# Residual stored into an accumulator over the gate's row, first registers loaded in batches, and another order between the feed-forward stage and the expert tiles

## What is computed

```python
sa, ca, ga, sb, cb, gb = (mod[:, 0], mod[:, 1], mod[:, 2], mod[:, 3], mod[:, 4], mod[:, 5])
ga = (2 * (ga >= 0) - 1) * jnp.maximum(jnp.abs(ga), 0.25)
gb = (2 * (gb >= 0) - 1) * jnp.maximum(jnp.abs(gb), 0.25)
h = _layernorm(x, axis=-1) * (1 + ca) + sa
x = x + ga * attn_ref(h, ...)
h = _layernorm(x, axis=-1) * (1 + cb) + sb
x = x + gb * ffn_ref(h, ...)
```

```python
scores = jax.nn.softmax(x @ gate_weight.T, axis=-1)
topk_weight, topk_idx = jax.lax.top_k(scores, TOP_K)
y = jnp.zeros_like(x)
for e in range(N_EXPERTS):
    w_e = jnp.sum(jnp.where(topk_idx == e, topk_weight, 0.0), axis=-1)
    y = y + w_e[:, None] * _glu_ffn(x, gate_up_weights[e], down_weights[e])
y = y + _glu_ffn(x, shared_gate_up, shared_down)
```

## Time and profile before

| | us |
|---|---|
| median of 3 runs (lowest, highest) | 366.6 (365.7, 367.72) |
| the profiled execution | 365.12 |
| its span in the profile | 363.3 |
| mean granted clock of TensorE | 0.948 |
| start of the first expert product (L1773) | 223.50 |

### The profile page before, as it was taken

The page is one execution under the profiler, slowest core; times in us unless marked ns, Lnnn a source line. Parts: engine busy times, 40 slices in busy tenths (PEclk is TensorE's granted clock), DMA queues, the critical chain, the costliest instruction groups (busy, mean ns, idle before and its releaser), DMA issues.

```text
span 363.3 us, 5639 instructions
## 1 busy us (share of the span) xinstructions
PE 317.4 (87%) x1424; PEld 236.1 (65%) x1424; DVE 209.1 (58%) x607; ACT 176.0 (48%) x338; POOL 162.8 (45%) x156
## 2 busy tenths in 40 slices
PE   6998989999999997999699787999999999999500
PEld 3785555766678876877497565777777777777300
DVE  4778998589576546594558834344343343343146
ACT  3488986798883533553271212443443444444200
POOL 3364487910001003256355571466566566666510
PEclk9889999999999999999988989999999999999855
DMA  6911031100019772002899464577766767765483
GB/s 206 359 68 59 1 115 59 60 0 0 2 48 361 158 144 73 2 17 98 231 321 325 150 204 157 111 111 108 121 113 105 115 118 109 120 113 62 56 231 133
DMA packets 43993, 44.91 MB, mean 124 GB/s; under 512 B 3387, under 2 KB 39995, under 8 KB 43963
## 3 DMA queue, kind: packets, MB, share of 16 engines
q1 hardware_dynamic: 35659, 33.66, 32.5%
q0 software_dynamic: 8304, 10.88, 18.7%
HBM read 27.74 MB, written 16.79 MB: 123 GB/s over the span
## 4 chain that ended last, share of the span: by engine, by line
PE 67%; DVE 15%; ACT 5%; DMA 5%; issue 4%; POOL 1%; SPq 1%; DVEq 0%; ACTq 0%; POOLq 0%
PE ps L1773 15%; PE ps L1800 10%; PE ps L1599 3%; PE ps L1361 3%; PE ps L1604 3%; PE ps L1600 3%; PE ps L1378 3%; PE ps L1362 3%; PE ps L1759 3%; PE ps L1786 3%; DMA acc_rows<-w,ids 2%; PE ps L1411 2%; PE ps L1418 1%; DVE w L1341 1%; DMA w<-in_wmod 1%
## 5 line engine op out<-in xcount | busy, mean ns | idle before, releaser
L546 POOL DMA_INDIRECT acc_rows<-w,ids x47 | 73.4, 1562 | 52.2 <-ACT w L866 49.6
L1773 PE MATMUL ps<-wup,w 128*128 x188 | 63.6, 460 | 1.5 <-DVE hm L1287 1.4
L1313 DVE TENSOR_TENSOR sg<-sg,ps 128x176 f32<-128x176 f32 x47 | 15.9, 338 | 68.4 <-ACT sg L858 68.4
L1800 PE MATMUL ps<-wdown,w 88*128 x188 | 48.6, 380 | 0.6 <-DVE w L1321 0.6
L533 POOL DMA_INDIRECT xs_rows<-h3x,slots x32 | 33.3, 1040 | 20.9 <-issue 20.9
L866 ACT ACTIVATE w<-ps,wv 128x256 f32<-128x256 f32 x47 | 22.3, 475 | 36.7 <-PE ps L1800 35.9
L1773 PEld LDWEIGHTS ps<-wup,w 128*128 128x128 f32 x188 | 32.0, 190 | 12.0 <-issue 1.9
L441 POOL TENSOR_TENSOR wsm_lo<-w,wsm_hi 128x512 fp32r<-128x512 f32 (+1 forms) x9 | 13.7, 1534 | 53.9 <-ACT wsm_hi L803 35.5
L1800 PEld LDWEIGHTS ps<-wdown,w 88*128 88x128 f32 x188 | 31.9, 190 | 3.8 <-issue 1.3
L858 ACT ACTIVATE sg<-ps 128x176 f32<-128x176 f32 x47 | 14.9, 317 | 33.3 <-PE ps L1773 33.3
L1599 PE MATMUL ps<-b_hi,wff_hi 128*128 128x512 f32 x64 | 26.9, 420 | 2.1 <-ACT w L756 1.3
(11 more groups left out here) (290 smaller groups left out, 705.9 us busy)
## 6 DMA issues: line engine op xcount, KB each, us to landing
xt<-xs_rows SPq DMA_DIRECT2D x47, 144.0 KB, 2.2
wup<-in_wmoe SPq DMA_DIRECT2D x4, 1408.0 KB
wdown<-in_wmoe SPq DMA_DIRECT2D x1, 2816.0 KB
xs_rows<-mod SPq DMA_DIRECT2D x17, 144.0 KB, 2.2
acc_rows<-mod SPq DMA_DIRECT2D x2, 1152.0 KB, 9.2
wdown<-in_wff SPq DMA_DIRECT2D x4, 512.0 KB, 6.4
w<-acc_rows SPq DMA_DIRECT2D x8, 256.0 KB, 4.6
w<-in_wsm SPq DMA_DIRECT2D x3, 512.0 KB, 9.2
```

Source lines behind the costliest of these rows:

```text
L546: nc.gpsimd.indirect_dma_start(acc_rows[n][:, :], bass.IndirectOffsetOnAxis(ids[:, i:i + 1], 0), ysb[i % YBUF], None, compute_op=ALU.add). ...
L1773: last = mm(bank(1, i)[:, 0:2 * FE].rearrange("p (w n) -> p w n", w=2), xT[i % 2][:, k * P:(k + 1) * P], up[:, k, :, bass.ds(e, FE)], star ...
L1800: last = mm(bank(3, i)[:, 0:C], hT[i % 2][:, h * P:(h + 1) * P], down[:, bass.ds(e + h * C, C)], start=h == 0, stop=h == 1)
```

## The change

1. The residual is no longer added at the end. VectorE takes the reciprocal of the gate's rows (`recip`), multiplies the tokens by it (`over`), adds the shared expert's output, now not scaled by the gate (`sum`, `finish`), and ScalarE's queue stores the two batches (512 KB each) into the second accumulator (`store_residual`), in step 2 of its tile loop. The second accumulation of the loop waits for this store. At the end VectorE adds the two accumulators and multiplies the sum by the gate's row: eight operations in place of sixteen.
2. The feed-forward weights lie by block (`wff_sb`), so the four loads of `wup` can start as their blocks come free: after block 2, block 5 and the last block of batch 1's up products, and after the last down product.
3. SyncE loads registers four at a time for the ends of the experts' rows (`empty_ends`) and for the first four tiles; TensorE loads its register of a tile before it waits for the tile's data.
4. The order of the middle is another (three plans), `st.1` and `finish.1` stand in step 1 of the tile loop, and the late table is cut into four pieces, one in each of the steps 1 to 4 of VectorE's tile loop. ScalarE's table loads are placed by `logset` and `siluset`. One scatter of batch 0 is cut in two, its first half ahead of `root.1.1`.

```diff
+UP_FREE = [3, 6, NF, NF]
...
 TENSOR_PLAN = """
...
-    ev.0.0 eg.0.1 t3.1 ev.0.1 logits.1 tx.1 eg.0.2 rank.1 edown.0.0 ev.0.2 edown.0.1 eg.1.0 ev.1.0 edown.0.2
+    ev.0.0 eg.0.1 eg.0.2 ev.0.1 t3.1 edown.0.0 logits.1 tx.1 ev.0.2 rank.1 edown.0.1 eg.1.0 edown.0.2 ev.1.0
...
+        rgb = mod[:, 1, 0:2, :]
...
-            sp.wait_ge(s("down_done"), NB * NF)
             for k in range(KC):
                 for which in range(2):
                     o = (2 * k + which) * P
+                    first_free = NF + UP_FREE[2 * k + which]
+                    sp.wait_ge(s("v2_psum"), first_free)
+                    if first_free == NB * NF:
+                        sp.wait_ge(s("down_done"), NF + 1 if which == 0 else NB * NF)
...
-            for e in range(NE // 2):
-                empty_end(e)
+            for e in range(0, NE // 2, 4):
+                empty_ends(e, e + 4)
             sp.wait_ge(s("tab_ready"), 2)
+            rows = [first_row(i) for i in range(RING)]
             sp.wait_ge(s("scattered"), 16 * (NB * NT - EARLY_T) * TOPK)
...
-                if i == 0:
-                    pool.wait_ge(s("filled"), 16 * NACC)
+                if i < 2:
+                    pool.wait_ge(s("filled"), 16 * (NACC + NB * i))
...
+                if i >= 2:
+                    act.wait_ge(s("prod_done"), SHARED[b] + i - 1)
...
+            def store_residual():
+
+                act.wait_ge(s("filled"), 16 * NACC)
+                for b in range(NB):
+                    act.wait_ge(s("tw_used"), 2 * NB + b + 1)
+                    act.dma_start(acc_rows[1][b * T:(b + 1) * T, :].rearrange("(t p) c -> p t c", p=P), hm[b][:, :, :]
+                                  ).then_inc(s("filled"), 16)
...
+                if step == 2:
+                    store_residual()
...
+            def recip():
+
+                dve.wait_ge(s("rows_sb"), 1)
+                dve.wait_ge(s("hn_ready"), 3)
+                at["recip"] = done(nc.vector.reciprocal(rgb, gbr[:, :, :]))
+
+            def over(b):
+
+                dve.wait_ge(s("hn2_ready"), NB + b + 1)
+                dve.wait_ge(s("dve_order"), at["recip"])
+                at["over", b] = done(nc.vector.tensor_tensor(hm[b][:, :, :], hm[b][:, :, :],
+                                                             rgb[:, b, :].unsqueeze(1).broadcast_to([P, NT, C]), ALU.mult))
...
+                if step == 1:
+                    finish(1)
                 if 0 <= step - 2 < NTILE:
                     ht_out(step - 2)
+                if step and step - 1 < len(late_table):
+                    late_table[step - 1]()
...
+            for b in range(NB):
+                for h in range(2):
+                    first, last = (tok(W[b][k])[:, 2 * h:2 * h + 2, :] for k in range(NACC))
+                    rows = hm[b][:, 2 * h:2 * h + 2, :]
+                    for k in range(NACC):
                         dve.wait_ge(*acc_in[(k * NB + b) * 2 + h])
+                    dve.wait_ge(s("filled"), 16 * (NACC + NB))
+                    link(nc.vector.tensor_tensor(first, first, last, ALU.add))
+                    nc.vector.tensor_tensor(rows, first, gbr[:, b, :].unsqueeze(1).broadcast_to([P, 2, C]),
+                                            ALU.mult).then_inc(s("y_ready"), 1)
...
             def tile_up(i):
 
+                pe.wait_ge(s("tab_ready"), 2 if i < EARLY else 3)
+                e = nc.tensor.value_load(tab[0:1, 1, i:i + 1], min_val=0, max_val=(NE - 1) * FE)
                 if i == 0:
                     pe.wait_ge(s("tw_used"), 2 * NB + 1)
```

More of the change, by code:

```diff
@@ L92 @@
     hn3.0 prod.1.2 h3.0 hidlo.1.2 prod.1.3 lgsub.0 hidlo.1.3 prod.1.4 topk.0 rank.0 h3lo.0 hidlo.1.4 pre.1
-    prod.1.5 hidlo.1.5 prod.1.6 hidlo.1.6 prod.1.7 hidlo.1.7 sum3.1 var3.1 hn3.1 egated.0.0 h3.1 egated.0.1
-    lgsub.1 elo.0.0 topk.1 rank.1 early elo.0.1 egated.0.2 h3lo.1 elo.0.2 need egated.1.0
-    late elo.1.0 egated.1.1 sum.0 finish.0 elo.1.1 egated.1.2 elo.1.2 sum.1 finish.1
+    prod.1.5 hidlo.1.5 prod.1.6 hidlo.1.6 recip prod.1.7 hidlo.1.7 sum3.1 var3.1 egated.0.0 hn3.1 elo.0.0 h3.1 egated.0.1
+    lgsub.1 elo.0.1 topk.1 rank.1 ends egated.0.2 h3lo.1 elo.0.2 early sum.0 over.0 egated.1.0 elo.1.0 finish.0
+    egated.1.1 elo.1.1 need over.1 egated.1.2 elo.1.2 sum.1
 """
@@ L531, in scatter @@
                     pool.wait_ge(s("slots_ready"), b + 1)
-                for k in range(TOPK):
+                for k in range(TOPK) if half is None else range(2 * half, 2 * half + 2):
                     nc.gpsimd.indirect_dma_start(
@@ L1593, in half_ff @@
             def half_ff(b, f, which, ready):
-                o = (2 * f + which) * P
+                hi, lo = (wff_sb[:, f, j, :, which * P:(which + 1) * P] for j in range(2))
                 out = PA(b)[:, which, :]
```

119 lines of the change are left out of this document (60 added, 59 removed).

## The result

| | before | after |
|---|---|---|
| median, us (lowest, highest) | 366.18 (365.7, 367.72) | 361.63 (360.12, 362.14) |
| executions | 4 | 4 |
| span of the profiled one | 363.3 | 360.3 |
| mean granted clock | 0.948 | 0.957 |

The ratio after to before is 0.9862, 95% interval [0.9819, 0.9905]: 4.6 us faster, where I had forecast 8.75.

A forecast was written before the change was run, and what follows sets the result against it. TensorE, busy 87% of the span, was taken as the bound, with gains only in its idle or half-speed middle and the tail. Terms summed to -8.75 us, from 366.6 to 357.8 us; range 353.5 to 362.5.

The forecast's parts named there:

- Reciprocal, +2.1: VectorE before `prod.1.7`: the new 128x512 reciprocal takes 4.2 us, less 2.12 us of idle cover, adding 2.1 us.
- TensorE fed, -2.65: During the second LayerNorm: two products placed ahead of `t3.1` fill TensorE's wait, saving 2.65 us.
- Clock, -1.7: After the wait before `t3.1`: the wait shrinks to 0.7 us, so the first low-clock stretch goes, saving 1.7 us.
- `eg.1.0`, +0.45: First shared gate of batch 1: TensorE waits 1.1 us for VectorE instead of 0.65, adding 0.45 us.
- `st.0`, -4.8: Transposes `st.0`: cutting up the late table removes the wait for VectorE's copy and a low-clock stretch, saving 4.8 us.
- Last down product, +0.65: Before the last shared down product: TensorE waits 1.6 us for VectorE and ScalarE, adding 0.65 us.
- `st.1` and the register load, -1.6: Before the first expert product: moving `st.1` and loading the tile register earlier remove waits, saving 1.6 us.
- First steps of the loop, +0.3, bounds 0 and 1.5: Start of the tile loop: VectorE's added `finish.1` and table pieces leave two short TensorE waits, adding 0.3 us.
- Tail, -1.5: After the last expert product: half of VectorE's sixteen operations go, saving 1.5 us, bounds -2.2 and 0.
- At nothing: Earlier `wup` loads, SyncE register batches, scatters moved ahead of `root.1.1` and the residual store: priced 0, store bounds 0 and 3.
- the third: Middle: scatters do not move, so tile loads hold TensorE back; 359.6 us, at most 361; chance 0.08.
- The second: Clock falls after the reciprocal's new wait before `down.1.7` and two more waits; 359.5 to 361.2 us; chance 0.15.

The follow-up runs named there:

- run with twelve: Changed kernel with four row ends emptied before the first tile loads instead of eight, so more stand before tile 4's load: 365.81 us, ratio 0.9958.
- orders, tuned: Changed kernel without its residual part, loads of tiles 4 to 8 put between the last emptyings, late table's pieces two steps later: 357.22 us, ratio 0.9777.
- all, tuned: Changed kernel, residual part kept, tile loads between emptyings, late table's pieces two steps later, reciprocal behind `hidlo.1.7`: 356.19 us, ratio 0.9647.
- orders-only run: Changed kernel with the residual part undone (no reciprocal, division, store or new tail), new orders and register batches kept: 361.57 us, ratio 0.9821.

## Why the prediction was right in sign and short in size

Seven steps behind `up.1.6`, against the profile after (less the 1.87 us by which it is late):

1. *Reciprocal, +2.1.* 3.35 us, not 4.2; `prod.1.7` came 1.05 later. Over-sized: the operation takes 6.4 copies of 523 ns, or 6.2 ns per element between the lengths 4 and 512. The Trainium skill (VectorE: DVE Perf Modes, the walkthrough of the 8-slice pipeline) gives a repeat count of 8, from which I had estimated eight copies, 4.2 us; the trace decides against that estimate.
2. *TensorE fed, -2.65.* Right: `eg.0.2` waits 0.78 (0.7 forecast), and between `down.1.7` and `t3.1` nothing waits longer.
3. *Clock, -1.7.* Right for the stretch named; the second one, behind the ranks, went too in this profile (1.00 from 184 to 195), and in seven of the twelve others with these orders, while five show it (down to 0.50). Worth up to 1.7 more.
4. *`eg.1.0`, +0.45.* It waits 0.91 against 0.65: +0.26.
5. *`st.0`, -4.8.* The wait and its low clock went, as said. What failed is what I took it to be worth.
6. *Last down product, +0.65.* It waits 1.11 against 0.78: +0.33.
7. *`st.1` and the register load, -1.6.* 1.41 became 0.54 and 0.70 went: right.

The first expert product, forecast near 212.5, started at 213.86 - 1.87 = 211.99. That replay of the orders was sound. The terms of my sum do not agree with it: they add to -7.55, the replay to 212.5 - 223.50 = -11.0, and I did not see that the two differ. Of the 3.96 us between -7.55 and the measured -11.51, 1.05 is the reciprocal, 1.7 the second stretch of low clock, which the replay at full clock leaves out and the sum keeps, and 0.9 `st.1`, which moved behind the product.

8. *First steps of the loop, +0.3, bounds 0 and 1.5.* **This is the term that failed:** 118.34 became 126.61, of which 0.9 is `st.1` moved in. The waits I named are there (0.32 and 1.06), but 3.09 us for tile 4 and about 2 us at 1.2 GHz are not in it, and 0.9 is not placed. I had written that nobody would wait for SyncE's batches of registers and that the tile loads had "some 2 us" of cover. I asked that of tile 0 alone, and there it was right (no wait for it). I did not count the queue on to tile 4: in the kernel before, that load went out 1.3 us behind the first product, and the middle was to pull that product forward by 11.
9. *Tail, -1.5.* From the issue of the last accumulation to the end it was 18.38 before and 17.45 after; in the experiments 18.68 twice with the old tail, and 16.85 to 17.92 in ten profiles with the new. Right.

```profile
342.85 1.55 POOL L556 DMA_INDIRECT acc_rows<-w,ids  x1 [0.32 <-issue]
```
```profile
352.31 0.69 DVE L1401 TENSOR_TENSOR w<-w,w 128x512 f32<-128x512 f32 x1 [14.02 <-DMA w<-acc_rows]
...
357.02 0.69 DVE L1402 TENSOR_TENSOR hm<-w,cB 128x512 f32<-128x512 f32 x1
```

10. *At nothing.* Wrong in both directions. The earlier loads of `wup` are worth about 2.3 us: without them the first tile loads go out 2.9 us later. The residual store, priced 0 with bounds 0 and 3, had its effect not on GpSimd, where I looked, but on SyncE's queue and tile 4: 3.7 to 4.0 us when it is left out, a part of it chance as said above. It landed 3.7 us after its issue (I had 5 to 9), some ten us before the second accumulation was issued (the first row is the page's, the others are of the timeline):

```profile
acc_rows<-hm ACTq DMA_DIRECT2D x2, 512.0 KB, 3.7
...
216.49 1.34 ACTq L863 DMA_DIRECT2D acc_rows<-hm  x2
...
232.02 1.60 POOL L556 DMA_INDIRECT acc_rows<-w,ids  x1 [6.99 <-DVE wv L1362]
```

No run undoes the register batches or the scatter cut in two, so what these two are worth stays open.

Of my rivals the third, tile loads become the bound, is what happened, at the fifth tile instead of the first; its 359.6 to 361 was short by the low clock. The second came true in the wrong place: the clock fell behind a wait of 3.09 us and not behind those of 1.13, 0.78, 0.91 and 1.11. The reciprocal was neither cheap nor dear, and nothing was given back at the accumulators. That 361.63 lies inside my range of 353.5 to 362.5 is in part luck: a loop that was wrong by 8 us was half hidden by a middle that gained 4 us more than my terms.

## What to carry to other kernels

Before a stage is pulled forward by ten microseconds, write down for every queue that feeds the next stage when its first dozen items leave, and not for the first one alone: the lead that hid them is what the change spends. A gain at one wait counts only up to where the next engine's queue stands, so terms of a sum that end at one and the same wait must be taken as a maximum. And a bulk transfer has its price on the queue of small loads beside it, if somebody waits for one of them.

## What the runs showed of the hardware

- RECIPROCAL of 128x512 takes 3.35 us, 6.4 times a copy of that shape.
- A register load on SyncE costs about 0.65 us when four stand together (2.6 us, from 211.35 to 213.95). The Trainium skill (DMA: Bandwidth & Descriptors, Latency and other measured facts) gives a floor of some 600 ns for `tensor_load`, which I take to be this load; the trace agrees. It depends on what else moves: eight DMAs with four register loads between them take 6.3 to 6.7 us with a quiet ScalarE queue and 7.3 to 8.1 beside a 1 MB store. Four of the DMAs take 1.95 us (first four of the run with twelve), so by my estimate a load takes 0.65 us in the first case (6.52) and 0.98 in the second (7.81).
- The "issue" before the first down product on TensorE is 0.45 and 0.51 us without the store, 1.06 to 1.31 with the whole store and the table's pieces in VectorE's first steps, and 0.63 to 0.68 with the store and the pieces elsewhere. So the store is not its only cause; what it waits for stays open.
- In three of fourteen profiles TensorE, ScalarE and SyncE stood still together for 3 to 7 us near the first tile loads, while the DMA engines were busy for 0.2 to 0.7 of the time and GpSimd's scatters went on. Nothing in these traces names what they waited for.
- From `up.1.6` to 240 us TensorE's granted clock stayed at 2.4 GHz behind the single waits of 0.7 to 1.52 us (the last in "orders, tuned") and was at 1.2 GHz behind those of 2.02 ("all, tuned"), 2.38, 2.62 us and all longer ones, and behind one pair of 1.78 and 0.66, for some 3 to 6.5 us. But single waits do not tell it all: in the orders-only run it was at 0.50 from 226 to 228 behind three short ones (0.51, 0.40 and 0.40), and the stretch behind the ranks, which has no wait ahead of it, is low in five of the thirteen profiles with the new orders and not in the other eight.
